# Retention scores from unsplit fp32 keys and queries, 32 rows to a head group, two groups to two banks by turns

## The reference, cut to what matters

```
def retention_forward(Q, K, V):            # Q = x after the first norm, K = V = ctx; B 8, S 256, 16 heads of 8
    q = _xpos(split(Q, HEAD), downscale=False)
    k = _xpos(split(K, HEAD), downscale=True)
    v = split(V, HEAD)
    D = _decay_mask(S, _gammas(HEADS))
    scores = jnp.einsum('bhsd,bhtd->bhst', q, k) * D[None]
    out = jnp.einsum('bhst,bhtd->bhsd', scores, v)
    return out.transpose(0, 2, 1, 3).reshape(B, S, HEADS * HEAD)
```

## Time and profile before

| | us |
|---|---|
| median of 3 runs | 809.16 (800.09 to 818.52) |
| profiled execution, its time | 808.52 |
| profiled execution, its span | 806.7 |
| PE busy | 647.5 (80%) |
| DVE busy | 468.5 (58%) |
| ACT busy | 368.2 (46%) |
| POOL busy | 283.4 (35%) |

### The profile page before, as it was taken

How to read it: one execution, slowest core, us unless ns; L and a number is a source line. 1 busy time by engine, 2 the same in 40 slices (tenths; PEclk the granted TensorE clock), 3 DMA queues, 4 the chain that set the end, 5 groups by cost and what they waited for, 6 DMA issues and landing times.

```text
span 806.7 us, 18948 instructions
## 1 busy us (share of the span) xinstructions
PE 647.5 (80%) x6549; PEld 497.2 (62%) x6549; DVE 468.5 (58%) x1730; ACT 368.2 (46%) x1283; POOL 283.4 (35%) x464
## 2 busy tenths in 40 slices
PE   5468988988998899869988997898899956762650
PEld 4345765675677678636776776576767845661650
DVE  2539538857974886557748766786566542431110
ACT  4344535545464665244646654554355432330230
POOL 0437214603921360359012601694400044305123
PEclk9768758985999999556999999898899966996795
DMA  4080300013044212040343241404342214665540
GB/s 141 12 306 2 100 1 2 19 70 109 21 133 128 91 38 87 24 141 8 114 129 109 75 152 40 148 16 168 118 120 73 74 66 153 204 187 165 158 129 23
DMA packets 47703, 77.71 MB, mean 96 GB/s; under 512 B 8240, under 2 KB 35064, under 8 KB 46456
## 3 DMA queue, kind: packets, MB, share of 16 engines
q1 hardware_dynamic: 45560, 72.30, 28.5%
q0 software_dynamic: 2048, 4.20, 1.6%
HBM read 64.45 MB, written 12.03 MB: 95 GB/s over the span
## 4 chain that ended last, share of the span: by engine, by line
PE 55%; issue 14%; DVE 14%; ACT 8%; POOL 6%; DMA 1%; SPq 0%; another core or an unknown queue 0%; DVEq 0%; POOLq 0%; ACTq 0%
PE bM L787 8%; PE bG L932 6%; PE bH L1159 6%; PE bR L1133 5%; PE bW L1133 4%; PE bM L975 4%; ACT ht L1373 4%; PE bS L951 3%; PE bM L980 3%; PE bC L1032 2%; PE bW L787 2%; PE bS L948 2%; PE bR L1064 2%; PE bG L1159 2%; PE bC L787 2%
## 5 line engine op out<-in xcount | busy, mean ns | idle before, releaser
L1373 ACT ACTIVATE ht<-bH,wt 128x128 f32<-128x128 f32 x216 | 61.5, 369 | 75.0 <-PE bH L1159 70.9
L1291 ACT ACTIVATE pp<-pp,nmx 128x224 f32<-128x224 f32 x96 | 46.4, 484 | 81.7 <-DVE nmx L1549 81.3
L1555 DVE TENSOR_TENSOR gs<-bG,rank_t 96x512 f32<-96x512 f32 x96 | 65.5, 682 | 15.1 <-PE bG L932 14.5
L1303 ACT COPY pts<-bM 128x256 f32<-128x256 f32 x96 | 35.4, 368 | 63.2 <-PE bM L787 62.8
L1618 DVE TENSOR_TENSOR sm<-bC,cst 128x512 f32<-128x512 f32 x64 | 43.6, 682 | 34.9 <-PE bC L1081 33.4
L1159 PE MATMUL bH<-xt,wt 128*128 128x128 f32 x432 | 62.8, 293 | 0.1
L932 PE MATMUL bG<-oh,kspl 128*96 128x512 f32 x160 | 61.3, 467 | 0.0
L693 POOL TENSOR_TENSOR r<-x,cst 128x256 f32<-128x256 f32 x8 | 5.8, 724 | 156.5 <-DVE x L1582 156.5
L1159 PEld LDWEIGHTS bH<-xt,wt 128*128 128x128 f32 x432 | 58.8, 209 | 1.0 <-issue 0.4
L1537 DVE TENSOR_SCALAR ppn<-pp,rls 128x224 f32<-128x224 f32 (+1 forms) x128 | 48.2, 376 | 14.1 <-DVE rls L1534 0.5
L975 PE MATMUL bM<-pts,ckw 96*32 96x64 f32 x512 | 52.4, 292 | 4.0 <-ACT ots L1311 4.0
(11 more groups left out here) (272 smaller groups left out, 1622.3 us busy)
## 6 DMA issues: line engine op xcount, KB each, us to landing
wt<-in_experts SPq DMA_DIRECT2D x67, 578.0 KB
sidx<-far_slots SPq DMA_DIRECT2D x8, 1536.0 KB, 6.6
xs<-sorted_tokens SPq DMA_DIRECT2D x67, 64.0 KB
expert_rows<-ot SPq DMA_DIRECT2D x67, 64.0 KB, 3.4
sorted_tokens<-acc SPq DMA_DIRECT2D x13, 256.0 KB, 7.7
cst<-shape_constants SPq DMA_DIRECT2D x1, 1603.5 KB, 6.3
xn<-in_x SPq DMA_DIRECT2D x8, 128.0 KB, 5.6
xr<-in_x SPq DMA_DIRECT2D x8, 128.0 KB, 3.3
```

Of the source, the lines that this page charges most:

```text
L1291: AC(pp[:, s % 2, 0:w], bS[:, 0:w] if s < T0 else pp[:, s % 2, :], ACT.Exp, scale=1.0 if s < T0 else -1.0, bias=nmx[:, s % 2:s % 2 + 1], a ...
L1373: last = AC(ht[:, t % 2, f, :], w[:, 128 * f:128 * f + 128], ACT.Relu, bias=wt[:, t % NW, FF + f:FF + f + 1])
L1555: TT(gs[:, g % 2, :].rearrange("p (t j) -> p t j", j=FAR), bG[0:96, :].rearrange("p (t j) -> p t j", j=FAR), rank_t[:, :].rearrange("p (o ...
```

## The change

Keys and queries are no longer split. PE turns each block of 128 tokens once: two flips of keys (`keys`, place 2) and two of queries (`queries`, place 5). ACT copies the keys as they are to `kT`, the second block of queries to `qT`, and both blocks to `qV` in four variants, in one go. A group's scores are now products of 32 rows of type fp32: its 32 feature rows lie at partitions 32g of `kT` and `qV`. At four places, each for a pair of groups, PE makes four matmuls of 256 columns, in the order group 0 into `bC`, group 1 into `bH`, and the same for the second half of the columns. DVE masks the two banks one after the other. Since `bH` is the experts' bank too, PE waits before a pair for the tile that last used it (`t_h`), and before a tile's first product for the masks of the pair that last used it (`c_freeV`), in `emptied_h`. The splits on DVE and their semaphores are gone. POOL waits, before it rotates the queries, for the last batch's `queries`.

```diff
-SCORES_AT = (5.5, 6, 7, 8, 9.5, 10.5, 11.5, 12.5)
+SCORES_AT = (6, 7.5, 10, 11.5)
...
-C_USES = (("out", "V"), ("keys0", "A"), ("state", "V"), ("keys1", "A"), ("query_dims", "A"), ("queries0", "A"),
-          ("scores0", "V"), ("scores1", "V"), ("scores2", "V"), ("scores3", "V"), ("queries1", "A"),
+C_USES = (("out", "V"), ("keys", "A"), ("state", "V"), ("queries", "A"),
+          ("scores0", "V"), ("scores1", "V"), ("scores2", "V"), ("scores3", "V"),
...
-        kS, qV = sb("kS", [128, 2, 4, 128], F32R), sb("qV", [128, 4, 4, 128], F32R)
+        kT, qV = sb("kT", [128, 2, 128]), sb("qV", [128, 4, 2, 128])
...
+            def emptied_h():
+
+                if "first" in held_h:
+                    pe.wait_ge(t_h.sem, t_h.at(held_h["first"], 1))
+                if "scores" in held_h:
+                    n, u = held_h["scores"]
+                    pe.wait_ge(c_freeV.sem, c_freeV.at(n, C_BY[:C_AT[f"scores{u}"] + 1].count("V")))
+                held_h.clear()
...
-                if s in (2, 3):
+                if s == 2:
+                    w = bank("keys")
+                    pe.wait_ge(r_k.sem, r_k.at(i.n, 1))
+                    for t in range(2):
+                        last = flip(w[:, 128 * t:128 * t + 128], rkn[:, t, :], 128)
                     full(last)
...
-                    u = SCORES_AT.index(s)
-                    t, g = u // 4, u % 4
-                    w = bank(f"scores{u}")
-                    full(MM(w[:, :], kS[:, t, g, :], qV[:, g, :, :], start=True, stop=True))
+                    pair = SCORES_AT.index(s)
+                    t = pair // 2
+                    emptied(f"scores{2 * pair - 2}" if pair else "queries")
+                    if pair == 0:
+                        pe.wait_ge(c_freeA.sem, c_freeA.at(i.n, 2))
+                    emptied_h()
+                    held_h["scores"] = i.n, 2 * pair + 1
+                    for half in range(2):
+                        for r in range(2):
+                            g = 2 * (pair % 2) + r
+                            last = MM((bC, bH)[r][:, 256 * half:256 * half + 256], kT[32 * g:32 * g + 32, t, :],
+                                      qV[32 * g:32 * g + 32, 2 * half:2 * half + 2, t, :], start=True, stop=True)
+                            if half == 1:
+                                full(last)
...
-                    if t >= 1:
-                        pe.wait_ge(t_h.sem, t_h.at(t - 1 if g < ALONE or t - 1 < FIRST_TILE[ALONE] else t - 2, 1))
                     w = first_bank(g, t)
+                    if w is bH:
+                        emptied_h()
+                        held_h["first"] = t
+                    elif t >= 2:
+                        pe.wait_ge(t_h.sem, t_h.at(t - 2, 1))
...
-                if s == 1:
-
-                    dve.wait_ge(r_k.sem, r_k.at(i.n, 1))
-                    dve.wait_ge(c_full.sem, c_full.at(i.n - 1, C_AT["keys1"] + 1))
-                    parts = rks[:, :, :, :, :].rearrange("p t g (a b) d -> p (t g) a b d", a=2)
-                    split(parts[:, :, 0, :, :], parts[:, :, 1, :, :], twice(rkn), r_ks, r_ks.at(i.n, 1))
...
-                    u = SCORES_AT.index(s)
-                    dve.wait_ge(c_av.sem, c_av.at(i.n, u // 4))
-                    full(f"scores{u}")
-                    free(TT(sm[:, u % 4, :].rearrange("p (v c) -> p v c", v=4), bC[:, :].rearrange("p (v c) -> p v c", v=4),
-                            C("causal").rearrange("p (o c) -> p o c", o=1).broadcast_to([128, 4, 128]), ALU.mult))
+                    pair = SCORES_AT.index(s)
+                    dve.wait_ge(c_av.sem, c_av.at(i.n, pair // 2))
+                    for r in range(2):
+                        full(f"scores{2 * pair + r}")
+                        free(TT(sm[:, 2 * (pair % 2) + r, :].rearrange("p (v c) -> p v c", v=4), (bC, bH)[r][:, :].rearrange("p (v c) -> p v c", v=4),
+                                C("causal").rearrange("p (o c) -> p o c", o=1).broadcast_to([128, 4, 128]), ALU.mult))
```

61 lines of the change are left out of this document (18 added, 43 removed).

## The result

| | before | after |
|---|---|---|
| median, us | 812.41 (800.09 to 818.52, 4 runs) | 824.86 (823.48 to 826.97, 4 runs) |
| profiled execution, us | 808.52 | 826.97 |
| span, us | 806.7 | 825.2 |
| PE busy / idle, us | 647.5 / 159.2 | 665.5 / 159.7 |

The ratio after to before is 1.024, with a 95% interval of 1.018 to 1.030. The change makes the kernel slower, by 12 us in the medians and by 19 in the ratio (15 to 24); the profiled executions stand 18.5 us apart. The ratio is of fast runs alone and leaves out the two slowest of before's four (815.66 and 818.52 us), which is why it says more than the medians. In the later rounds before has medians of 808.9 to 814.6, which would put after's 824.9 at 1.3 to 2.0% above it. The forecast was 798 with a range up to 812, so it missed on the side that had a chance of 0.11. Idle time in the table is span less PE's busy time.

The account below looks back on a forecast made before the run. PE's own work was taken to bound the kernel, with other engines counting where PE waits. Gains of 18.7 us less 2.8 more work and 4.5 and 0.8 new waits gave 10.6 us, so 798 us from 808.5; overall range 782 to 812.

Parts of the forecast that it names:

- freer engines and a clock that comes back sooner: Rival on stretches at 1.2 GHz: a quarter of their PE work runs at 2.4 GHz, 11 us more gained, 787 us; chance 0.27.
- 18.7 us of waits: PE's waits that go: keys 6.0, kS 2.8, queries 4.1, qV 1.9, masks 1.5, last batch's qV filling 2.4 us.
- A pair, 0.96 us: New score products on PE: four 32-row matmuls of 256 columns take 0.96 us a pair, 30.7 us for 32.
- the third rival: New score pairs: groups do not run side by side, a pair costs 1.98 us, time 831 us; chance 0.11.
- Two pairs at 1.2 GHz: Batch 3's half-clock stretch: two of 32 score pairs lie there and add 1.9 us.
- Keys, 6.0 us: PE's wait for split keys: without the split the norm's root begins about 0.75 us sooner, in 8 batches, 6.0 us gained.
- Queries, 4.1 us: PE's wait for split queries: of 15.9 us only 4.1 gained, since DVE stays late in batches 1, 3 and 5.
- Three masks ahead of a tile, 4.5 us: Tiles right behind a score pair: three times PE waits 1.5 us for both masks, 4.5 us lost.
- Last batch, 2.4 us: Last batch: the second filling of qV, on the chain with 2.43 us, no longer exists; 2.4 us gained.
- the 0.7 us for DVE's backlog: Two masks ahead of stage B's maximum at four slots: costed at nothing, 0.7 us each if DVE has a backlog.
- the second rival: PE waits later for the same DVE or POOL work: half of 18.7 us is lost, time 807 us; chance 0.18.
- Flips, 14.4 us less: PE's flips of keys and queries: 17 a batch become 4, so 104 go, 14.4 us less work.

Follow-up runs that it names:

- three pairs of kernels: After and its 64-row form, each plain, with one more flip of keys, and with ACT's order changed: ratios 1.024, 1.010, 1.018 against 0.998, 0.992, 0.998.
- the kernel with 64 rows: After, but pairs use 64 rows by turns, with keys written twice and every other group's rows set to zero: 806.3 us, ratio 0.998.
- The kernel with neither flips nor splits: After, but kT and qV are fp32r and a group's scores are one product of 128 rows and 512 columns: 787.3 us, ratio 0.973.
- 32 full products of another kind, the filler: After, with a useless fp32 product of 128 rows and 256 columns ahead of each pair of scores: 835.1 us, ratio 1.033.
- its three kernels: After itself, after with one more flip of keys, and after with ACT's order changed: 824.9, 823.9 and 828.4 us; ratios 1.024, 1.010, 1.018.
- the three kernels on either side: After's three 32-row kernels, average ratio 1.017; three with fp32r products of 128 rows (one plain, two with four key copies), average 0.977.
- fp32r products by turns: After and the kernel with 64 rows, each with kT and qV declared fp32r: 803.0 and 801.9 us, ratio 0.988 for both.
- the doubled pair: After, with the four products of every pair made twice: 833.5 us, ratio 1.033.
- the pair of full height: After, but each pair's four fp32 matmuls use all 128 rows of kT and qV: 811.8 us, ratio 1.004.

## Why the prediction was wrong, step by step

**The step that failed** is the clock. The sum priced the new pairs by their duration alone and left PE's clock as it was but for two pairs. The only case on the clock, "freer engines and a clock that comes back sooner", had the wrong sign. In its place: fp32 products by turns that use half the array's height let the clock fall to 1.2 GHz behind them, where products of the same length that use all of it, with the same waits around them, do so less often (8 of 9 against 1 of 9 at a tile that waits 1.53 us). This costs some 17 us (32 against 64 rows, three pairs of kernels).

**The second step that failed** is the overlap of the waits. The sum took 18.7 us of waits as gone and put stage B's new ones at nothing; PE's idle time stayed, which is 13.9 us of the miss. Even the kernel with 64 rows, without the clock's loss, is at 806 (0.998) and not at 798.

Term by term, on the profiled executions (808.5 to 827.0, where 10.6 less was forecast, a miss of 29 us):

- *A pair, 0.96 us.* Measured 1.06 in the median, 2.01 at 1.2 GHz. The rows on 64-row products gave 0.16 us for 64 more columns; measured it is 0.22 (1.93 - 1.06 for 256 columns). The strips do run side by side, as this piece of batch 4 shows (437.05 to 438.11), so the third rival, which gave 831 us for pairs of 1.98, had about the time and the wrong cause:

```profile
437.05 0.48 PE L1086 MATMUL bC<-qV,kT 32*128 32x256 f32 x1
437.05 0.48 PE L1086 MATMUL bH<-qV,kT 32*128 32x256 f32 x1
437.37 0.37 PE L1086 MATMUL bC<-qV,kT 32*128 32x256 f32 x1
...
438.11 0.46 PE L954 MATMUL bS<-kd,qall 128*128 128x96 f32 x2
```

- *Two pairs at 1.2 GHz.* Of the 32 pairs 23 lie wholly at 2.4 GHz, 8 at 1.2 and one across a change. With the length above this makes 23 x 1.06 + 8 x 2.01 + 1.5 = 42 us instead of 32.6: 9 us of the miss. The other work that now lies at 1.2 GHz makes the rest of PE's busy time: 18.0 - 2.8 - 9.4 = 5.8 us. The records of the clock agree: from 55 us on PE is busy at 1.2 GHz for 175.3 us instead of 149.6, which is 12.9 us of time, and has 5.5 us more work. The forecast's 104.5 us at 1.2 GHz, with 88.1 of busy PE, were stretches of batches 0 to 3 only; from 55 us on the kernel before has 211.5 us, with 149.6.
- *Keys, 6.0 us.* In batch 4 the mechanism was right to the hundredth. From `y` to the root of the norm it was 418.23 - 415.44 = 2.79 us, and is 420.88 - 418.83 = 2.05. Before (the root is in the earlier trace rows), then after:

```profile
415.44 0.42 DVE L1594 TENSOR_TENSOR y<-bC,xr 128x256 f32<-128x256 f32 x1 [2.39 <-PE bC L1032]
...
418.46 0.63 PE L787 MATMUL bC<-cst,rks 128*128 128x128 f32 x4 [1.76 <-DVE rks L1455]
...
419.84 1.13 PE L1133 MATMUL bR<-wt,ht 128*128 128x128 f32 x8 [0.56 <-DVE taken L1677]
```

```profile
418.83 0.42 DVE L1592 TENSOR_TENSOR y<-bC,xr 128x256 f32<-128x256 f32 x1 [2.39 <-PE bC L1038]
...
420.88 0.16 DVE L1571 SCALAR_TENSOR_TENSOR lnv<-lnv 128x2 f32<-128x2 f32 x1 [0.50 <-ACT lnv L1330]
...
422.19 0.17 DVE L1665 TENSOR_TENSOR taken<-bR,cst 128x8 f32<-128x8 f32 x1
...
422.50 1.32 PE L1141 MATMUL bR<-wt,ht 128*128 128x128 f32 x6 [2.00 <-DVE taken L1665]
```

  PE now stands 2.00 us for the router's marks, where it stood 1.76 for the split and 0.56 for the marks. In sum 13.2 us for `rks` went and 9.6 came for `taken`, which leaves 3.6 of the 6.0.
- *Queries, 4.1 us.* 15.9 us went, and `rb`, which waits for the same late work of DVE's, grew from 2.3 to 13.3: 4.9 us. Right.
- *Three masks ahead of a tile, 4.5 us.* Measured 4.6, 1.5 at most. Right.
- *Last batch, 2.4 us.* Wrong: PE's wait for the transfer there grew from 4.0 us to 7.9.
- *Not counted:* stage B's own waits. `nmx` grew by 2.6 us, `pp` by 4.8, that transfer and the experts' `ht` by some 7. The forecast had the 0.7 us for DVE's backlog in its text and then at nothing. With these, idle time came out at +0.5 us instead of -13.4. This is the second rival, "the stalls move", which had half of the 18.7 us as lost, and more than half was: 13.9 us of the miss. Together 9.4 + 5.8 + 13.9 = 29.
- *But idle time was not the only place to look for the splits' price.* Without splits, and nothing else changed, the time falls by 26 us, and of the 15.9 us between the profiled executions 13.7 are in PE's busy time, through the clock. So the waits' sum of 18.7 us was no overestimate of what the splits cost; most of it stood in the wrong account, and the right one was not watched.
- *Flips, 14.4 us less.* As work this arrived, as time it did not. The kernel with neither flips nor splits, with pairs of the old form, has 13.9 us less work than the one without splits alone (529.5 and 543.4). But its ratio is no lower (0.973 and 0.968): it has more of its work at 1.2 GHz (130.5 and 121.1 us), 2.4 us more idle time, and the pairs' coupling, which cost before 9 us (3 to 15). And 96 flips more on after cost 2 us. The forecast cited "TensorE: Matmul & The Clock Gate" (Part 4) of the Trainium skill, by which transposes do not count as activity, as a reason that fewer of them lift the clock. No run here shows that: with 96 more flips PE's work at 1.2 GHz stayed as it was (174.5 us against 175.3), and with fewer it did not fall (130.5 against 121.1). The first would fit the rule, but 32 full products of another kind left it as it was too (174.6), so the runs do not tell.

In ratios, the change is: splits out -26 us; flips out, pairs and shared bank +4 (forecast some -18); old form to 32 rows +41. Sum +19. After's own ratio is the highest of its three kernels, and the last step is +32 by the averages of the three kernels on either side. As work, 20 of it are found (24 pairs x 0.51 and 8 x 1.01), where the forecast had 32.6 - 15.4 = 17.

**Left open.** How height and time add up for the clock: doubling the 32-row products gave 11.5 us back through it, and fp32r products by turns show no difference between 32 and 64 rows. One number per pair does not reproduce all ratios. Whether the wait of 1.5 us behind the pair is needed for the fall is not shown: no run keeps the 32 rows and takes the wait away. Of the drain that "TensorEngine Tiling (Array Packing)" (Tiling Modes) of the Trainium skill speaks of, only a sum is shown: a pair of 1.06 us holds 0.87 us of products (what the doubled pair adds) and 0.19 us more, where the pair of full height, 1.73, is 4 x 0.43 with nothing over. That the 0.19 us are this drain is a reading of it.

## What to carry to other kernels

Where PE's granted clock is below full in parts of a profile, price a change of PE's work twice: by duration, and by how much of the array it leaves in use. A shorter or equal instruction stream that uses fewer rows can lose more in the clock behind it than it saves. Look first at the places where PE waits right behind such products. And a wait that goes away can return as idle time elsewhere and still pay, or not pay, through the clock; compare busy time at equal work before crediting idle time. Compare clocks only over stretches in which both traces have records of it.

## What the runs showed of the hardware

- Two strips of 32 rows and two of 64 rows take the same time for four fp32 products of 256 columns (1.06 us; 2.01 at 1.2 GHz), against 1.73 at full height. With fp32r: 0.43 us for either.
- At equal work and waits, 32 rows instead of 64 cost some 17 us of 810 in the ratios. In the profiles PE was busy at 1.2 GHz for 178 us on average instead of 148, and 22 of the 31 us between them lie right behind the three pairs that a waiting tile follows. The rows that 64 has more hold zeros in one operand.
- Work added to PE was partly paid back. By the clock, 11.5 of 28 us of doubled pairs, and 29 us against 22 us of work for full height, which made the kernel 13 us faster. As less idle time alone, 4.7 us of the flips' and 4.9 of the filler's.
- A change of no work (the order of ACT's copy and its four variants) moved the ratio by 0.000 to 0.021, up to 17 us.
